# Tile 3 of batch 0 last in the first half of a quantized product: a new order on four engines

## What is computed

```
q1 = clip(round(layernorm(x) / s1 + z1), 0, 255)      # per batch: 512 rows x 1024
q2 = clip(round(ctx / s2 + z2), 0, 255)               # per batch: 1024 x 1024
x  = x + tanh(g_xattn) * s1 * s2 * (q1 - z1) @ (q2 - z2)
x  = x + tanh(g_ffn) * ffn(layernorm(x))              # base linear + 8 gated adapters of rank 16
```

## Time and profile before

| | us |
|---|---|
| median of 3 runs (lowest, highest) | 183.38 (182.61, 183.68) |
| the profiled execution | 184.68 |
| its span in the trace | 182.9 |
| PE busy | 173.2 (95%) |
| DVE busy | 115.2 (63%) |
| ACT busy | 90.8 (50%) |
| POOL busy | 72.3 (40%) |

### The profile page before, as it was taken

How to read it: one execution, slowest core, us unless ns; L and a number is a source line. 1 busy time by engine, 2 the same in 40 slices (tenths; PEclk the granted TensorE clock), 3 DMA queues, 4 the chain that set the end, 5 groups by cost and what they waited for, 6 DMA issues and landing times.

```text
span 182.9 us, 2896 instructions
## 1 busy us (share of the span) xinstructions
PE 173.2 (95%) x1058; PEld 150.6 (82%) x1058; DVE 115.2 (63%) x281; ACT 90.8 (50%) x123; POOL 72.3 (40%) x89
## 2 busy tenths in 40 slices
PE   4669999999999999999999999999999999999993
PEld 4565644768899999999964479999999999999993
DVE  0787886989878988887798654492551351351303
ACT  2179760485796965378710106133790880820300
POOL 3263002870101186286699999036410500500220
PEclk9996999999999999999999999999999999999999
DMA  6999999799430052045232000004407207102003
GB/s 213 332 390 388 383 409 411 243 378 387 154 117 3 30 200 115 4 86 118 87 61 115 0 0 0 4 0 92 138 0 142 91 0 162 69 4 115 2 0 115
DMA packets 19934, 25.39 MB, mean 139 GB/s; under 512 B 11207, under 2 KB 12615, under 8 KB 19920
## 3 DMA queue, kind: packets, MB, share of 16 engines
q1 hardware_dynamic: 19906, 25.21, 41.1%
q10 hardware_dynamic: 14, 0.00, 0.0%
HBM read 18.39 MB, written 4.19 MB: 123 GB/s over the span
## 4 chain that ended last, share of the span: by engine, by line
PE 88%; DVE 4%; DMA 3%; ACT 3%; issue 1%; ACTq 1%; POOL 0%
PE bank L1045 19%; PE bank L1047 19%; PE bank L1046 19%; PE bank L923 15%; PE bank L1005 3%; DMA rt<-in_L_xattn_x_zp_dram 3%; PE bank L1033 2%; PE bank L1069 2%; PE bank L1071 2%; PE bank L1070 2%; PE bank L981 2%; DVE st L662 1%; ACT WTh L509 1%; PE bank L909 1%; DVE q L684 1%; ACT q1u L476 1%
## 5 line engine op out<-in xcount | busy, mean ns | idle before, releaser
L1045 PE MATMUL bank<-WTh,lnTh 128*128 128x388 f32 (+3 forms) x192 | 67.3, 350 | 0.3 <-DVE lnTl L730 0.3
L1047 PE MATMUL bank<-WTh,lnTl 128*128 128x388 f32 (+3 forms) x192 | 65.1, 339 | 0.0
L1046 PE MATMUL bank<-WTl,lnTh 128*128 128x388 f32 (+3 forms) x192 | 65.0, 339 | 0.0
L1045 PEld LDWEIGHTS bank<-WTh,lnTh 128*128 128x128 f32 x192 | 36.1, 188 | 1.2 <-DVE lnTl L730 0.6
L1046 PEld LDWEIGHTS bank<-WTl,lnTh 128*128 128x128 f32 x192 | 36.2, 189 | 0.3
L1047 PEld LDWEIGHTS bank<-WTh,lnTl 128*128 128x128 f32 x192 | 36.2, 188 | 0.3
L437 POOL TENSOR_TENSOR xs<-xs,tb 128x1024 f32<-128x1024 f32 x8 | 19.3, 2418 | 39.4 <-ACT xs L491 39.4
L923 PE MATMUL bank<-q,q1T 128*128 128x512 bf16 x128 | 31.4, 391 | 0.2 <-DVE q L697 0.2
L923 PEld LDWEIGHTS bank<-q,q1T 128*128 128x128 bf16 x128 | 12.5, 100 | 14.6 <-issue 0.7
L431 POOL TENSOR_TENSOR xs<-xs,colbc 128x512 f32<-128x512 f32 x14 | 18.1, 1318 | 15.6 <-DVE xs L716 12.2
L662 DVE BATCH_NORM_STATS2 st<-xs 128x6 f32<-128x512 f32 x32 | 20.8, 684 | 5.1 <-DMA xs<-in_x_dram 4.2
(11 more groups left out here) (102 smaller groups left out, 233.1 us busy)
## 6 DMA issues: line engine op xcount, KB each, us to landing
xs<-in_x_dram SPq DMA_DIRECT2D x8, 512.0 KB, 7.2
landing<-in_ctx_dram SPq DMA_DIRECT2D x8, 512.0 KB, 10.8
ring<-in_ctx_dram SPq DMA_DIRECT2D x8, 512.0 KB, 6.1
out_dram<-xs SPq DMA_DIRECT2D x7, 512.0 KB, 2.9
ring<-in_L_ffn_W_base_dram SPq DMA_DIRECT2D x4, 512.0 KB, 12.5
landing<-in_L_ffn_W_base_dram SPq DMA_DIRECT2D x4, 512.0 KB, 15.3
ring<-in_L_ffn_A_w_dram SPq DMA_DIRECT2D x1, 512.0 KB, 12.4
ring<-in_L_ffn_B_w_dram SPq DMA_DIRECT2D x1, 512.0 KB, 4.1
```

Source lines behind the costliest of these rows:

```text
L1045: mm(o, hi, WTh[:, k, a:b], start=(k == 0), stop=False, skip_group_check=True)
L1046: mm(o, hi, WTl[:, k, a:b], start=False, stop=False, skip_group_check=True)
L1047: ins = mm(o, lo, WTh[:, k, a:b], start=False, stop=(k == KT - 1), skip_group_check=True)
```

## The change

Tile 3's statistics, rounding, transposition and products move behind other work. DVE copies tile 0's transposition ahead of `round_q1(1)`, and takes tile 3's statistics in two pieces after `round_ctx(1)`. ACT does context chunk 1 ahead of tile 2, and chunks 3 and 4 ahead of tile 3. PE does the column steps of chunks 0 and 1 ahead of tile 2's products, and goes through the chunks with tiles 0 to 2 first and with tile 3 at the end. The first column sum goes to bank 7 and the second to bank 6, and tile 3's transposition to bank 6. `row_term(0)` moves behind `round_ctx(6)` on DVE, since its input is complete later, and PE's wait for it moves from ahead of the second half to the first use of bank 2 in that half.

```diff
-    flips = [("q1", t) for t in range(MT)] + [("rows", 0), ("cols", 0, 0), ("cols", 0, 1)] + early
+    flips = [("q1", t) for t in range(MT)] + [("cols", 0, 0), ("rows", 0), ("cols", 0, 1)] + early
...
+        elif key in (("q1", 3), ("cols", 0, 0), ("cols", 0, 1)):
+            i = 7 if key == ("cols", 0, 0) else 6
+            n_alternate += 1
...
             affine_ctx(0)
+            affine_ctx(1)
             affine_q1(2)
-            affine_ctx(1)
-            affine_q1(3)
             affine_ctx(2)
...
-            for c in range(3, CPB):
+            affine_ctx(3)
+            affine_ctx(4)
+            affine_q1(3)
+            for c in range(5, CPB):
                 affine_ctx(c)
...
             ln_moments(0, 2, (1,))
-            ln_moments(0, 3)
+            copy_q1T(0)
             round_q1(1)
-            copy_q1T(0)
             round_ctx(0)
             copy_q1T(1)
+            round_ctx(1)
+            half_stats(0, 3, 0)
             round_q1(2)
-            round_ctx(1)
+            ln_moments(0, 3, (1,))
             copy_q1T(2)
-            round_q1(3)
             round_ctx(2)
-            copy_q1T(3)
+            round_ctx(3)
...
-            round_ctx(3)
+            round_q1(3)
+            round_ctx(4)
+            copy_q1T(3)
+            round_ctx(5)
+            round_ctx(6)
             row_term(0)
-            for c in range(4, CPB):
-                round_ctx(c)
+            round_ctx(7)
...
+                        if b == 0 and (k2, m) == (0, 1):
+                            pe.wait_ge(row_terms, 1)
...
             product_chunk(0, (0, 1))
-            flip_q1(2)
             product_chunk(1, (0, 1))
             row_sums(0, (0, 1))
-            flip_q1(3)
+            flip_q1(2)
+            column_step(0, 0)
+            column_step(0, 1)
             product_chunk(0, (2,))
             product_chunk(1, (2,))
             row_sums(0, (2,))
-            product_chunk(0, (3,))
-            product_chunk(1, (3,))
+            product_chunk(2, (0, 1, 2))
+            column_step(0, 2)
+            flip_q1(3)
+            product_chunk(3, (0, 1, 2))
+            column_step(0, 3)
+            for k2 in range(CPH):
+                product_chunk(k2, (3,))
             row_sums(0, (3,))
-            for k2 in range(CPH):
-                column_step(0, k2)
-                if k2 >= 2:
-                    product_chunk(k2, range(MT))
-            pe.wait_ge(row_terms, 1)
```

## The result

| | before | after |
|---|---|---|
| median of 17 runs, us | 183.46 (182.50 to 183.88) | 182.32 (182.06 to 183.63) |
| the profiled execution, its span, us | 184.68, 182.9 | 183.32, 181.5 |

The account below looks back on a forecast made before the run. PE bounds it, 95% busy, losing time only at its early lull and the slow clock behind it. -0.66 - 0.40 - 1.67 + 1.50 = -1.23 us, so 183.38 becomes 182.2; range 181.3 to 183.6.

Parts of the forecast that it names:

- Start: DVE rounds tile 1 earlier, so PE's second transposition starts at 13.21 instead of 13.87: -0.66 us.
- First products: PE's first products: ready at 14.01, started at 15.07 before, chunk 1's data costing ACT nothing: -0.40 us.
- Clock: PE's first eight products and one transposition run at the full clock, 2.19 instead of 3.86 us: -1.67 us.
- the rival in which the clock falls again: PE's clock still falls behind the shortened first gap: 182.9, or 183.4 with nothing left; chance 0.34.
- New waits: PE stands 0.19 and 0.15 in first products, 0.32 for tile 2's copy, 0.84 ahead of tile 3's transposition: +1.50 us.
- Tile 3 and POOL: POOL's three steps for tile 3, the new weak point, take 2.29 us; PE waits 0.84 at its transposition.
- the long price: POOL's three steps for tile 3 take 2.29 us, as beside DVE's roundings and copies, rather than 1.35.
- the low end of the sum: With POOL's short price, DVE's constants hold tile 3's rounding; PE waits 0.52 instead of 0.84, sum -1.55 us.
- The rest: Remaining matmuls of the half take the same 7.75 us; what is won by the second half's entry reaches the end.
- DVE's used-up cover: DVE's later adds eat its 2.10 us idle at 32.32 without costing PE; a later DVE would.
- The sum: All terms up to PE's second-half entry, at 25.84 instead of 27.08: -1.23 us.

Follow-up runs that it names:

- e2: Changed kernel with 7 more idle matmuls behind tile 0's transposition (keep_busy(13) for keep_busy(6)): 182.52 us, ratio 0.9952 to the kernel before.
- e8: Changed kernel with tile 3's transposition moved behind chunk 3's products of tiles 0 and 1: 181.77 us, ratio 0.9912 to the kernel before.
- e5: Changed kernel with DVE's eight constants moved behind tile 3's rounding and copy: 182.21 us, ratio 0.9941 to the kernel before.
- e9: e8 with 7 more idle matmuls behind tile 0's transposition, as in e2: 181.81 us, ratio 0.9907 to the kernel before.
- e11: Same kernel as e9, run on another chip beside the changed kernel: 181.86 us, ratio 0.9925 to the kernel before.
- e1: Kernel before, old order, with 14 more idle matmuls behind tile 0's transposition: 182.50 us, ratio 0.9958 to the kernel before.
- e4: Changed kernel with tile 3's statistics back ahead of tile 1's rounding on DVE: 183.75 us, ratio 1.0009 to the kernel before.
- e7: Changed kernel without both groups of six idle matmuls behind the transpositions of tiles 0 and 1: 183.00 us, ratio 0.9966 to the kernel before.
- e3: Kernel before with only tile 3's statistics moved on DVE, behind tile 0's copy and tile 1's rounding: 183.89 us, ratio 1.0026 to the kernel before.

## Why the prediction was right, step by step

Right was the size (1.14 measured, 1.2 forecast), the place, and that the clock is most of it. The terms are less right than their sum. By its own steps:

*Start*, -0.66. From the first to the second transposition it was 3.10 before and is 2.45 in the changed kernel, in e2 and in e8: **-0.65**.

*First products*, -0.40 more. Short of it, in some executions: from the first transposition to the first product it was 4.30 before, 3.24 was forecast, and the full-clock traces have 3.77 (e5), 3.58 (e2), 3.39 (e8), 3.25 (e9) and 3.24 (e11). I had the chunks' data cost ACT nothing. The timeline of ACT in e8 shows what it does: ACT waits 0.16 for the transfer of chunk 0, and the two chunks one after the other take 2.52. In e11 the data is there: no wait, 2.36 for the two, and the term as forecast.

```profile
11.07 2.52 ACT L487 ACTIVATE q2u<-landing,prm,con 128x1024 uint8<-128x1024 f32 x2 [0.16 <-DMA landing<-in_ctx_dram]
```

*Clock*, -1.67, "the step with the least support". The direction held, and e1, e4 and e7 show the cause; the rival in which the clock falls again is recorded in none of the 29 executions. It is not seen in the changed kernel's own two traces, where PE was slow until 15.9; it is seen in e5's, which is the same program up to tile 3 and runs at the full clock from 9.81 on. The size was wrong: in e1, where nearly nothing else changes, the stretch is only 0.84 shorter (16.31 to 15.47). The eight products and one transposition do shrink, from 3.86 to 2.45 (14.21 to 16.66 in e1's trace), but PE then stands for what the slow clock had hidden, such as the 0.47 ahead of the first products (0.24 before).

*New waits*, +1.50, were too many, and that made up for it: 0.22 in the first products (1.95 instead of 1.73), 0.23 for tile 2's copy and 0.49 ahead of tile 3 make 0.94 in e2, against 0.34, 0.32 and 0.84. Clock and waits are one term rather than two: from the first product to the second half's entry before took 12.01, the forecast has 11.83, e2 11.61.

*Tile 3 and POOL.* I took the long price, 2.29 (13.21 to 15.50; 2.20 of it from the first step's start). In the changed kernel's trace POOL has the short one instead: 16.90 to 18.16, 1.26, as for tile 2 in the earlier trace rows (11.61 to 12.87). POOL, then DVE:

```profile
16.90 0.55 POOL L401 TENSOR_TENSOR cf<-cf,mhalf 128x1 f32<-128x1 f32 x1 [4.59 <-DVE cf L680]
17.52 0.19 POOL L404 TENSOR_TENSOR cf<-cf,con 128x1 f32<-128x1 f32 x1
17.82 0.34 POOL L405 TENSOR_SCALAR cf<-cf,prm 128x1 f32<-128x1 f32 x1
```

```profile
17.52 0.69 DVE L655 COPY q1T<-bank 128x1024 bf16<-128x1024 bf16 x1 [0.71 <-PE bank L917]
...
20.67 0.15 DVE L809 TENSOR_SCALAR con<-con 128x1 f32<-128x1 f32 x1
20.86 0.69 DVE L689 TENSOR_SCALAR q<-q1u 128x1024 bf16<-128x1024 uint8 x1
```

DVE stood waiting for PE, and only its copy out of PSUM ran beside the three steps. Tile 3's rounding then came right behind the constants, as in the low end of the sum. In e2, with the clock up, DVE didn't stand, and POOL took 1.93; POOL, then DVE in the same microseconds:

```profile
16.59 0.55 POOL L401 TENSOR_TENSOR cf<-cf,mhalf 128x1 f32<-128x1 f32 x1 [4.37 <-DVE cf L680]
17.22 0.54 POOL L404 TENSOR_TENSOR cf<-cf,con 128x1 f32<-128x1 f32 x1
17.86 0.66 POOL L405 TENSOR_SCALAR cf<-cf,prm 128x1 f32<-128x1 f32 x1
```

```profile
16.43 0.68 DVE L655 COPY q1T<-bank 128x1024 bf16<-128x1024 bf16 x1
17.02 1.29 DVE L702 TENSOR_SCALAR q<-q2u 128x1024 bf16<-128x1024 uint8 x2
```

The first step, beside the copy, keeps its 0.55; the other two, beside the roundings, take 0.54 and 0.66 instead of 0.19 and 0.34. So both ends occur, by what DVE runs, and the wait came out nearer the low end of 0.52 than 0.84: 0.49 in e2. The Trainium skill's exclusive lock ("SBUF — State Buffer", section "Who interferes with whom") agrees: the copy held none of the three steps, the roundings two. So the rule had the operations right, and the number of its end. The way to that number was another: POOL's 1.93 is nearer to 2.20 than to 1.26, and DVE waited for ACT (0.23 ahead of the rounding at 19.95), not for the constants. That 0.49 lies at the low end is luck.

*The rest* held: 155.8 behind the second half's entry in both. The bank swap, the later row terms and DVE's used-up cover cost PE nothing: between 31 and 42 us it stood 0.17 and 0.34 us, both as before (the prediction passed over the 0.17, which stands at 39.42 there). That DVE's idle time of 2.10 would be used up also held; in the changed kernel the add has none ahead of it:

```profile
30.32 0.69 DVE L667 BATCH_NORM_STATS2 st<-xs 128x6 f32<-128x512 f32 x1
30.96 0.69 DVE L730 TENSOR_TENSOR xs<-xs,colbc 128x512 f32<-128x512 f32 x1
```

*The sum.* At the full clock the changed order takes 15.19 in e2, so -1.12 against -1.23 forecast. The terms alone were -0.65 - 0.07 + (-0.40), where the forecast had -0.66 - 0.40 - 0.17. So two misses, 0.33 less gain than forecast in the first products and 0.23 more in clock and waits, nearly cancel, and that the total is so near is partly luck. In e5, where chunk 0's data came 0.45 late, the stretch is 15.54, only 0.77 less than before.

## What to carry to other kernels

A lull can cost more than its own length: here a clock that fell behind it cost another 0.7 us (e7). A few idle matmuls in it may do what a reordering does; test that first, as in e1. Work that comes late needs a late place with its consumer too: tile 3's statistics paid only with PE's new order (e3), and the next 0.5 us were had by moving its transposition two more tiles back (e8). And price a gain in clock together with the waits that it uncovers: forecast apart, at -1.67 and +1.50, the two came to -0.40 in e2 and not to -0.17.

## What the runs showed of the hardware that was not expected

- A granted clock of 1.00 in the page, in the windows and in a run's mean can stand for "nothing recorded yet". In two traces of the changed kernel eight transposing matmuls took 1.03 to 1.06 us under a printed 1.00; in the first of them the next eight, at 16.88, took 0.61. The time of the same small matmul group is the surer clock.
- When the clock first rises differs between executions of programs that are the same up to there: between the first and second transposition in e8's trace (1.06, then 0.62; first record at 10.96), at 9.81 in e5's, at 15.9 in both profiled executions of the changed kernel. The stretch of 16.02 there against 15.19 in e2 suggests that this is what its executions of 183 us and more (6 of 29) have in common; it was seen in the two that were profiled, and for the others it stays open. That the filler in e2, e9 and e11 keeps them away by an earlier rise was not traced in enough executions to call it shown.
- Tile 0's start differs by about 1.1 us between profiled executions (10.77 in one, 9.4 to 9.7 in eleven), with the arrival of the parameters. Spans of single profiles differ by as much as this whole change.
